# Graph attention on one core: steps of 1024 edges in plain edge order, maxima by a segmented scan

## The chip, the core and the metric

The kernel runs on one core of one Trainium2 chip. A core has five engines that work side by side and meet at semaphores: TensorE (PE; its weight loads are listed apart as PEld), VectorE (DVE), ScalarE (ACT), GpSimd (POOL) and SyncE (SP), which here only issues transfers. The metric is the device time of a run in microseconds; less is better.

## The reference

There are 6250 nodes with 64 features and 206250 edges, sorted by target node `dst`. After a message-passing layer come two graph attention layers of this form (4 heads of 32 channels, then 1 head of 64):

```python
def _gat_layer(x, src, dst, W, a_src, a_dst, b, heads, ch, concat):
    h = (x @ W).reshape(n, heads, ch)
    alpha_src = jnp.sum(h * a_src, axis=-1)
    alpha_dst = jnp.sum(h * a_dst, axis=-1)
    e = alpha_src[src] + alpha_dst[dst]
    e = jnp.where(e > 0, e, NEG_SLOPE * e)
    alpha = _segment_softmax(e, dst, n)
    msg = h[src] * alpha[:, :, None]
    out = jax.ops.segment_sum(msg, dst, num_segments=n)
    return out + b
```

The first part, unchanged but for small pieces, computes per edge `silu(silu([x[src], x[dst], edge_attr, w] @ ew1 + eb1) @ ew2 + eb2)`, sums it by node and applies a small network to the node.

## The kernel before

Nodes stand in 49 buckets of 128, one node on each partition. Edges are worked off in groups of `GE` = 512 edges of one bucket, `U` = 4 on each partition; since each bucket is padded to whole groups there are `GROUPS` = 452.

The program has stages: ordering and placing the edges (to about 450 us), storing the edges' first products at their places by source (`bring` and `put`, to about 2400), the edge network (`edge_mlp`, to about 3950), the node network, and the two attention layers. Each layer is a software pipeline, `attention_pipeline`: every engine has its own `attend(of)`, in which `of(k)` is the group that entered k steps before. Sixteen steps are written out, the rest is a loop with eight steps a round; all engines run through the same number of steps, each at its own pace, and only semaphores hold them together. What an engine does within a step is in the order in which `attend` is written.

For one group of layer 1 the work is as follows.

- SyncE loads the group's ids (`load_ids`). GpSimd gathers the rows of the source nodes from `table0` in HBM with four indirect transfers of 128 rows each (`gather_rows`, L689), into a ring of eight.
- VectorE makes lane numbers and their bits (`edge_codes`, L1464 to L1481) and writes 16 codes beside each gathered row. ScalarE makes from the lane numbers the one-hot matrix edge to node, `a_hot` (L825, L832), and a copy of it in fp32, `a_hot_f` (L857).
- TensorE transposes `a_hot` (L1064) and the codes with the three bf16 parts of the source's shares (L1069), when the rows have landed; ScalarE copies both out of PSUM (L849, L851). A matmul of 512 columns for each head (L1110, `pick`) then shows on every node's partition the shares of its own edges and a very large negative number for all others, and VectorE reduces these to the maxima (`largest_shares`, L1494 in layer 1, L1490 in layer 2).
- VectorE computes the new running shift of the bucket (`new_shifts`, ten short operations), TensorE looks it up for each edge (L1081, twelve small matmuls), VectorE makes the logits (`logits`, four operations), ScalarE the exponentials (L839), VectorE the messages (`messages`, L1580).
- TensorE sums the messages by node with four fp32 matmuls (L1093) of 132 columns, 65 in layer 2; VectorE shrinks the old sum of the bucket and adds the new one (`sums`, L1592 and L1597). The sum goes into one PSUM bank, so each waits until the one before is added (`a_added`).

Semaphores that matter below: `a_hot_ready` (ScalarE), `turned` and `looked_up` (TensorE), `logit_step`, `msg_ready` and `a_added` (VectorE), `exp_ready` (ScalarE).

## Time and profile before

| | us |
|---|---|
| median of 3 runs | 11986.1 |
| lowest and highest | 11957.8, 12015.4 |
| span of the profiled execution | 8886.9 |
| median less span | 3099.2 |
| layer 1 of attention, about | 4062 to 6454 |
| layer 2 of attention, about | 6536 to 8867 |

The span goes from the first to the last instruction that the trace shows. The profile gives no total time of the profiled execution, so the difference to the median is what lies outside its instructions, together with whatever differs between executions. Busy shares are means over stages with different limits, so each stage is read by itself. A clock of 1.00 is TensorE's upper level, 0.50 the lower; values between are a mix in time.

### The profile page before, as it was taken

To read this page: it belongs to the slowest core of one execution; us is meant where nothing else is said; L and a number is where in the kernel's file an instruction comes from. 1 tells how busy PE (TensorE), PEld (TensorE's weight loads), DVE (VectorE), ACT (ScalarE), POOL (GpSimd) and SP (SyncE) were. 2 spreads that over 40 slices of the span, in tenths; PEclk is the share of its full clock that TensorE was granted. 3 is DMA by queue.
4 is the path that set the end of the run, shared out by engine and by line. 5 is a ranking of instruction groups with operands and counts; after the bars stand their busy time and mean duration, and the time that the engine had idled before them with its cause. 6 is when DMAs were issued, how large, how long until landed. Compare 5 with 4: busy or idle time off the path is not lost.

```text
span 8886.9 us, 230055 instructions
## 1 busy us (share of the span) xinstructions
PE 6173.7 (69%) x49885; PEld 5210.5 (59%) x50563; DVE 6168.8 (69%) x25428; ACT 4847.6 (55%) x11854; POOL 6191.5 (70%) x7562
## 2 busy tenths in 40 slices
PE   2466666666599999984666666666646666666665
PEld 2365656556588888873555555545445555656564
DVE  7799833333267676757999999999856666666665
ACT  4133333333245555534777777777647777777775
POOL 0377777777777777735777777777647777777775
PEclk9988888888899999986888888888755555555555
DMA  4233222222232323312222222222421111111114
GB/s 141 52 63 63 62 63 62 63 62 62 61 90 85 86 85 86 85 35 56 55 55 55 55 55 55 56 55 56 47 25 29 29 29 29 29 29 29 29 29 28
DMA packets 990923, 493.64 MB, mean 56 GB/s; under 512 B 830674, under 2 KB 841604, under 8 KB 990276
## 3 DMA queue, kind: packets, MB, share of 16 engines
q0 software_dynamic: 168832, 302.29, 15.6%
q1 hardware_dynamic: 701892, 169.48, 10.2%
q10 hardware_dynamic: 119840, 18.68, 1.3%
q14 instruction: 329, 2.70, 0.1%
q8 instruction: 30, 0.49, 0.0%
HBM read 356.53 MB, written 151.48 MB: 57 GB/s over the span
## 4 chain that ended last, share of the span: by engine, by line
issue 26%; POOL 21%; PE 20%; DVE 15%; DMA 7%; ACT 7%; DVEq 3%; ACTq 1%; POOLq 0%; SPq 0%; another core or an unknown queue 0%
POOL z_s L639 13%; POOL arena L689 8%; DMA arena<-table,arena 6%; PE ps_all L961 5%; PE ps_all L971 5%; ACT arena L825 3%; PE ps_all L984 3%; PE ps_all L981 2%; DVE arena L1494 2%; PE ps_all L1069 1%; ACT arena L857 1%; DVE arena L1580 1%; PE ps_all L993 1%; DVEq L385 1%; DVE ps_all L1232 1%
## 5 line engine op out<-in xcount | busy, mean ns | idle before, releaser
L689 POOL DMA_INDIRECT arena<-table,arena x3616 | 3527.3, 975 | 1421.4 <-issue 963.9
L639 POOL DMA_INDIRECT z_s<-arena x1660 | 1591.9, 959 | 850.8 <-issue 479.6
L1093 PE MATMUL ps_all<-arena 128*128 128x132 f32 (+1 forms) x7232 | 1584.7, 388 | 1.8 <-DVE acc L1597 1.8
L1093 PEld LDWEIGHTS ps_all<-arena 128*128 128x128 f32 x7232 | 1405.9, 288 | 2.7 <-issue 2.6
L1069 PE MATMUL ps_all<-ident_b,arena 128*128 128x128 bf16 x3616 | 465.3, 270 | 1311.8 <-DMA arena<-table,arena 1191.7
L825 ACT ACTIVATE arena<-lanes_b,arena 128x128 bf16<-128x128 bf16 x3616 | 1144.9, 386 | 349.1 <-DVE arena L1467 342.2
L1069 PEld LDWEIGHTS ps_all<-ident_b,arena 128*128 128x128 bf16 x3616 | 282.3, 117 | 1478.6 <-issue 844.4
L1494 DVE TENSOR_REDUCE arena<-ps_all 128x2 f32<-128x1024 f32 x904 | 1098.5, 1215 | 39.0 <-PE ps_all L1110 37.6
L849 ACT ACTIVATE arena<-ps_all 28x512 bf16<-28x512 bf16 (+1 forms) x904 | 527.5, 584 | 956.8 <-PE ps_all L1069 955.8
L744 ACT ACTIVATE arena<-ps_all 18x512 f32<-18x512 f32 x415 | 243.3, 586 | 1211.9 <-PE ps_all L948 1180.1
L1110 PE MATMUL ps_all<-arena,pick 128*128 128x512 bf16 x1809 | 694.6, 489 | 54.6 <-DVE arena L1494 24.3
L1332 DVE CAST arena<-arena 128x4 f32<-128x4 int32 x415 | 72.9, 176 | 875.9 <-DMA z_s<-arena 874.9
L768 ACT ACTIVATE arena<-arena 128x512 f32<-128x512 f32 x452 | 284.9, 630 | 704.6 <-DVE arena L1364 704.6
L946 PE MATMUL ps_all<-ident_b,arena 128*128 128x128 bf16 x1660 | 175.3, 232 | 660.4 <-DVE arena L1325 657.6
L931 PE MATMUL ps_all<-w_edge,arena 128*128 128x128 f32 x3320 | 603.5, 340 | 11.6 <-issue 11.3
L1364 DVE TENSOR_TENSOR arena<-ps_all,b_mid 128x512 f32<-128x512 f32 x452 | 312.4, 691 | 430.5 <-PE ps_all L971 430.5
L1064 PEld LDWEIGHTS ps_all<-ident_b,arena 128*128 128x128 bf16 x3616 | 388.3, 128 | 378.1 <-issue 302.4
L1064 PE MATMUL ps_all<-ident_b,arena 128*128 128x128 bf16 x3616 | 479.9, 274 | 155.9 <-ACT arena L832 106.0
L832 ACT ACTIVATE arena<-arena 128x512 bf16<-128x512 bf16 x904 | 568.8, 629 | 30.6
L931 PEld LDWEIGHTS ps_all<-w_edge,arena 128*128 128x128 f32 x3320 | 532.5, 243 | 72.5 <-issue 43.1
L857 ACT ACTIVATE arena<-arena 128x512 f32<-128x512 bf16 x904 | 553.3, 612 | 0.0
L934 PE MATMUL ps_all<-arena 128*128 x3320 | 545.1, 319 | 0.0
(259 smaller groups left out, 15032.7 us busy)
## 6 DMA issues: line engine op xcount, KB each, us to landing
arena<-z_s SPq DMA_DIRECT2D x452, 264.0 KB, 2.7
arena<-table,arena POOLq DMA_INDIRECT x3616
arena<-rec_d SPq DMA_DIRECT2D x1660, 10.0 KB
z_s<-arena POOLq DMA_INDIRECT x1660
rec_d<-in_rec ACTq DMA_DIRECT2D x1, 16160.0 KB, 59.0
arena<-ids_d SPq DMA_DIRECT2D x904, 4.0 KB
arena<-pos_d SPq DMA_DIRECT2D x830, 0.5 KB
arena<-pos_d ACTq DMA_DIRECT2D x830, 0.5 KB
```

Source lines behind the costliest of these rows:

```text
L639: pool.indirect_dma_start(z_s, bass.IndirectOffsetOnAxis(ap=slot[:, g.slot(SLOTS), u:u + 1], axis=0), z_out[:, g.slot(SLOTS), u, :], None) ...
L689: pool.indirect_dma_start(g_rows[:, r, u * step + CODE_WORDS:(u + 1) * step], None, tables[n], bass.IndirectOffsetOnAxis(ap=ids[:, r, 0, u ...
L825: act.activation(lane_gap[:, g.slot(2), u, :], lanes_b, ACT.Square, bias=neg_lane[:, g.slot(4), u:u + 1]).then_inc(S("lane_gap_ready"), 1)
L832: act.activation(a_hot[:, g.slot(SLOTS)], lane_gap[:, g.slot(2)], ACT.Relu, scale=-1.0, bias=1.0).then_inc(S("a_hot_ready"), 1)
L857: act.activation(a_hot_f[:, g.slot(4)], a_hot[:, g.slot(SLOTS)], ACT.Copy).then_inc(S("a_hot_f_ready"), 1)
L931: pe.matmul(ps[2 + r][:, u * P:(u + 1) * P], x_t[:, g.slot(4), u * P:(u + 1) * P], w_edge, start=(u == 0), stop=False, skip_group_check=True)
L934: mm = pe.matmul(ps[2 + r][:, u * P:(u + 1) * P], own_hot[:, g.slot(4), u, :], own_dst[:, bass.ds(tiles[u], 1), :].rearrange("p a f -> p ( ...
L1064: pe.transpose(bank[:, u * P:(u + 1) * P], a_hot[:, r, u, :], ident_b)
L1069: mm = pe.transpose(bank[:, GE + u * P:GE + (u + 1) * P], g_rows[:, r, u * step:u * step + P // 2].bitcast(BF16), ident_b)
L1093: mm = pe.matmul(ps[6][:, 0:out_w], a_hot_f[:, g.slot(4), u, :], g_msg[:, g.slot(4), u * out_w:(u + 1) * out_w], start=(u == 0), stop=(u = ...
L1110: mm = pe.matmul(bank, picks[n][:, h, :], turned[:, g.slot(SLOTS), 1, :], start=True, stop=True)
L1494: dve.tensor_reduce(part_max[:, g.slot(4), 2 * pair:2 * pair + 2], ps_all[:, pair * 1024:(pair + 1) * 1024].rearrange("p (h e) -> p h e", ...
```

## The change

The edges are no longer padded by bucket. They are taken in plain order in 202 blocks of `BLOCK` = 1024, two halves of 512, `AU` = 8 edges on each partition. A block that holds edges of two buckets is visited once for each; a step of the pipeline is such a visit of block and bucket, `VISITS` = 202 + 48 = 250 a layer. Edges of another bucket have an all-zero row in `a_hot` at that visit.

- SyncE and GpSimd now run by blocks: eight gathers each, into a ring of eight blocks. GpSimd itself waits for the landing of a block, after two gathers of the next, and raises `blocks_in`. SyncE reuses a slot when the last visit of its block is through (`msg_ready`). The node number of each edge stays in SBUF for both layers (`node_of`); before, it was loaded each time.
- In layer 1 codes and `pick` matmuls are gone. VectorE copies the gathered shares (`gathered_shares`), TensorE turns them into 8 rows, half and head, of 512 edges (L1182), VectorE runs a segmented maximum along them (`scan_shares`, L1671, `tensor_tensor_scan` with flags that are very negative at the first edge of a node), TensorE turns the result back (L1194), VectorE keeps it at the last edge of each node (`segment_ends`, L1681), and eight fp32 matmuls of 4 columns bring it to the nodes' partitions (L1218). The flags are computed once, on VectorE in the edge network's stage (`edge_flags`), stored, and read back two transfers a step on ScalarE's queue (`load_flags`).
- Layer 2 keeps codes and `pick`, in 1024 edges at a time.
- The pipelines are shorter: messages four steps behind the start instead of six, and one-hot matrices, transposes and shrink factors have four slots instead of eight, messages two instead of four.

```diff
+AU = HALVES * U
+BLOCK = HALVES * GE
+BLOCK_BITS = 10
+BLOCKS = STORED // BLOCK
+VISITS = BLOCKS + NT - 1
+RING = 8
...
+    return 2 if heads == 1 else 0
...
+        a_hot_f, at = carve(at, [4, AU, P])
+        slot_words = AU * row_words(*LAYERS[0])
+        g_rows, at = carve(at, [RING * slot_words])
+        g_msg, at = carve(at, [2, AU * (F_HID + HEADS)])
...
+                def landed(k):
+
+                    pool.wait_ge(S(f"gathered_{k.slot(LANDING)}"), k.uses(LANDING, 16 * AU))
+                    pool.sem_inc(S("blocks_in"), 1)
...
+                    for u in range(AU):
+                        if u == 2 and k.back(1).exists():
+                            landed(k.back(1))
                         pool.indirect_dma_start(
-                            g_rows[:, r, u * step + CODE_WORDS:(u + 1) * step], None, tables[n],
-                            bass.IndirectOffsetOnAxis(ap=ids[:, r, 0, u:u + 1], axis=0)
-                        ).then_inc(S(f"gathered_{r}"), 16)
-
-                attention_pipeline(pool, 0, gather_rows, n)
+                            g_rows[:, r * slot_words + u * row:r * slot_words + (u + 1) * row], None, tables[n],
+                            bass.IndirectOffsetOnAxis(ap=ids[:, r, u:u + 1], axis=0)
+                        ).then_inc(S(f"gathered_{k.slot(LANDING)}"), 16)
...
+                    g = of(-1)
+                    if n == 0 and g is not None:
+                        load_flags(g)
...
+                        if n == 0:
+                            pe.wait_ge(S("parts_ready"), g.done())
+                            if g.back(1).exists():
+                                pe.wait_ge(S("scanned"), g.back(1).done())
+                            by_u = ps[0][0:HALVES * heads, :].rearrange("k (p u) -> k p u", u=U)
+                            for u in range(U):
+                                mm = pe.transpose(by_u[:, :, u], shares[:, r, u, :], ident)
+                            mm.then_inc(S("shares_turned"), 1)
...
+                    g = of(2)
+                    if g is not None and n == 0:
+                        k = HALVES * heads
+                        pe.wait_ge(S("scanned"), g.done())
+                        if g.back(1).exists():
+                            pe.wait_ge(S("ends_ready"), g.back(1).done())
+                        pe.sem_inc(S("go"), 1)
+                        by_u = running[0:k, g.slot(2), :].rearrange("k (p u) -> k p u", u=U)
...
+                            mm = pe.transpose(ps[1][:, u * k:(u + 1) * k], by_u[:, :, u], ident[0:k, 0:k])
+                        mm.then_inc(S("scan_turned"), 1)
...
+                        for u in range(AU):
+                            mm = pe.matmul(ps[6][:, 0:out_w], a_hot_f[:, g.slot(4), u, :], g_msg[:, g.slot(2), u * out_w:(u + 1) * out_w],
+                                           start=(u == 0), stop=(u == AU - 1))
                         mm.then_inc(S("a_summed"), 1)
...
-                            bank = ps[h] if heads > 1 else ps[g.slot(2)]
-                            mm = pe.matmul(bank, picks[n][:, h, :], turned[:, g.slot(SLOTS), 1, :], start=True, stop=True)
-                            if h % 2 == 1 or heads == 1:
-                                mm.then_inc(S(f"shown{h // 2}"), 1)
...
+                        if n == 0:
+                            pe.wait_ge(S("ends_ready"), g.done())
+                            pe.wait_ge(S("a_hot_f_ready"), g.done())
+                            for a in range(HALVES):
+                                for u in range(U):
+                                    mm = pe.matmul(ps[2][:, a * heads:(a + 1) * heads], a_hot_f[:, g.slot(4), a * U + u, :],
+                                                   largest[:, g.slot(2), u, a * heads:(a + 1) * heads], start=(u == 0), stop=(u == U - 1))
+                        else:
+                            pe.wait_ge(S("codes_turned"), g.fresh().done())
+                            for a in range(HALVES):
+                                mm = pe.matmul(ps[a], pick, turned_codes[:, g.slot(2), a * GE:(a + 1) * GE], start=True, stop=True)
+                        mm.then_inc(S("shown"), 1)
...
+                def gathered_shares(g):
 
...
+                        dve.wait_ge(S("shares_turned" if n == 0 else "turned"), g.back(4).done())
+                    rows = rows_of_visit(g)
+                    dve.wait_ge(S("blocks_in"), (block_of(g) & COUNT_MASK) + (n * BLOCKS + 1))
+                    dve.sem_inc(S("go"), 1)
+                    if n == 0:
+                        dve.tensor_copy(shares[:, r].rearrange("p u (a h) -> p a u h", a=HALVES),
+                                        rows.rearrange("p (a u w) -> p a u w", a=HALVES, u=U)[:, :, :, at_s:at_f]).then_inc(S("parts_ready"), 1)
...
+                def scan_shares(g):
...
-                    for pair in range(heads // 2):
-                        dve.wait_ge(S(f"shown{pair}"), g.done())
-                        dve.tensor_reduce(part_max[:, g.slot(4), 2 * pair:2 * pair + 2],
-                                          ps_all[:, pair * 1024:(pair + 1) * 1024].rearrange("p (h e) -> p h e", h=2),
-                                          op=ALU.max, axis=AX.X).then_inc(S(f"max_taken{pair}"), 1)
-                        yield
+                    k, r = HALVES * heads, g.slot(2)
+                    dve.wait_ge(S(f"flags_in{g.slot(4)}"), g.uses(4, 16 * HALVES))
+                    if g.back(2).exists():
+                        dve.wait_ge(S("scan_turned"), g.back(2).done())
+                    dve.wait_ge(S("shares_turned"), g.done())
+                    dve.tensor_tensor_scan(running[0:k, r, :], flags[0:k, g.slot(4), :], ps[0][0:k, :], -BIG, ALU.add, ALU.max
+                                           ).then_inc(S("scanned"), 1)
...
+                def segment_ends(g):
+
+                    if g is None or n == 1:
+                        return
+                    if g.back(2).exists():
+                        dve.wait_ge(S("shown"), g.back(2).done())
+                    dve.wait_ge(S("scan_turned"), g.done())
+                    dve.scalar_tensor_tensor(largest[:, g.slot(2)].rearrange("p u (a h) -> p (u a) h", a=HALVES),
+                                             ps[1][:, 0:AU * heads].rearrange("p (u h) -> p u h", h=heads), low,
+                                             edges_of_visit(is_last, g).unsqueeze(2).broadcast_to([P, AU, heads]), ALU.subtract, ALU.mult
+                                             ).then_inc(S("ends_ready"), 1)
...
-                    ahead = of(-1)
-                    codes = edge_codes(of(0), ahead) if ahead is not None and ahead.off % 2 == 1 else iter(())
-                    large, shifts = largest_shares(of(3)), new_shifts(of(4))
-                    logs, adds = logits(of(6)), sums(of(8))
-                    for part in (shifts, codes, logs, shifts, adds, logs, shifts, codes, logs, shifts, adds, logs,
-                                 large, shifts, large, shifts):
+                    shifts, logs, adds, codes = new_shifts(of(3)), logits(of(4)), sums(of(6)), edge_lanes(of(0))
+                    for part in (logs, shifts, codes):
                         next(part, None)
-                    messages(of(6))
-                    for part in (shifts, codes, shifts):
+                    segment_ends(of(2))
+                    for part in (logs, shifts, codes, logs, shifts, adds, logs, shifts, codes, adds, shifts):
                         next(part, None)
-
-                attention_pipeline(dve, 8, attend, n, buckets.load)
-                dve.wait_ge(S("a_added"), GROUPS * (n + 1))
+                    scan_shares(of(1))
+                    for part in (shifts, shifts):
+                        next(part, None)
+                    largest_shares(of(2))
+                    messages(of(4))
+                    gathered_shares(of(0))
```

TensorE in attention layer 1 of the kernel before, one step of 512 edges in the steady loop (`ident_b` marks the bf16 transposes, `pick0` the code table, `128x132` the summing matmuls):

```order
L1110 MATMUL ps_all<-arena,pick0 128x512
L1110 MATMUL ps_all<-arena,pick0 128x512 [waits max_taken1]
L1110 MATMUL ps_all<-arena,pick0 128x512
L1062 REGISTER_ALU [waits turned_copied]
L1064 MATMUL ps_all<-ident_b,arena 128x128 [waits a_hot_ready]
L1064 MATMUL ps_all<-ident_b,arena 128x128 x3
L1069 MATMUL ps_all<-ident_b,arena 128x128 [waits gathered_5,high_code_ready,low_code_ready]
L1069 MATMUL ps_all<-ident_b,arena 128x128 x3
L1075 REGISTER_ALU
L1077 REGISTER_ALU [waits max_step]
L1081 MATMUL ps_all<-arena 128x8 [waits logit_step]
L1081 MATMUL ps_all<-arena 128x8 x11
```

TensorE in layer 1 of the changed kernel, one step of 1024 edges (L1182 turns the shares, L1194 turns the scan back, L1205 sums, L1218 is the 4-column matmul that shows the maxima, L1235 the lookups):

```order
L1162 REGISTER_ALU [waits turned_copied]
L1174 MATMUL ps_all<-ident_b,tab 128x128 [waits a_hot_ready]
L1174 MATMUL ps_all<-ident_b,tab 128x128 x7
L1182 MATMUL ps_all<-ident,arena 8x128 [waits scanned,parts_ready]
L1182 MATMUL ps_all<-ident,arena 8x128 x3
L1194 MATMUL ps_all<-ident,arena 128x8 [waits scanned,ends_ready]
L1194 MATMUL ps_all<-ident,arena 128x8 x3
L1205 MATMUL ps_all<-arena 128x132 [waits a_added,msg_ready,a_hot_f_ready]
L1205 MATMUL ps_all<-arena 128x132 x7
L1218 MATMUL ps_all<-arena 128x4 [waits a_hot_f_ready,ends_ready,max_taken]
L1218 MATMUL ps_all<-arena 128x4 x7
L1229 REGISTER_ALU [waits turned_copied]
```

Moved: the four `pick0` matmuls of 512 columns are gone; two groups of fp32 transposes stand before the sum and eight fp32 matmuls of 4 columns behind it, and the transposes no longer wait for the gather but for `parts_ready` and `scanned`, which VectorE raises.

VectorE in layer 1 before, from the last logit steps to the two reductions of 1024 columns:

```order
L1568 TENSOR_TENSOR arena<-arena,ps_all 128x16 [waits logit_step]
L1507 REGISTER_ALU
L1531 TENSOR_TENSOR arena<-shift,arena 128x4 [waits max_step]
L1532 CAST arena<-arena 128x4
L1597 TENSOR_TENSOR acc<-acc,ps_all 128x132 [waits a_shrunk,a_summed]
L1552 REGISTER_ALU
L1571 TENSOR_SCALAR arena<-arena 128x16 [waits logit_step]
L1494 TENSOR_REDUCE arena<-ps_all 128x2 [waits shown0]
L1507 REGISTER_ALU
L1535 TENSOR_SCALAR shift<-arena 128x4 [waits max_step]
L1536 TENSOR_TENSOR arena<-arena 128x4
```

VectorE in layer 1 of the changed kernel, from the end of one step (L1656 copies the gathered shares) to `segment_ends` of the next (L1681):

```order
L1656 ISA
L1656 COPY arena<-arena 128x2x4x4
L1758 TENSOR_TENSOR arena<-arena,ps_all 128x32 [waits looked_up]
L1718 ISA [waits shrink_ready,looked_up]
L1718 TENSOR_SCALAR arena<-dst_parts 128x3x4
L1720 ISA [waits max_taken]
L1720 TENSOR_TENSOR arena<-arena,alpha_d 128x4
L1623 ISA [waits a_hot_ready]
L1623 ISA
L1623 TENSOR_TENSOR arena<-first_node,arena 128x8
L1681 ISA [waits scan_turned,shown]
L1681 SCALAR_TENSOR_TENSOR arena<-ps_all,low,arena 128x32
```

Moved: the reductions of 1024 columns (L1494) are gone from the step; a step now opens with the first logit operation and, two short operations on, stands at L1681 until TensorE has turned the scan of the same step (`scan_turned`).

## Rows read from the trace of the kernel before

**Rows 1.** the page: busy us and share by engine; tenths of 40 slices

```profile
PE 6173.7 (69%) x49885; PEld 5210.5 (59%) x50563; DVE 6168.8 (69%) x25428; ACT 4847.6 (55%) x11854; POOL 6191.5 (70%) x7562
...
POOL 0377777777777777735777777777647777777775
PEclk9988888888899999986888888888755555555555
```

**Rows 2.** stretches of both layers: PE, PEld, DVE, ACT, POOL busy, granted clock, DMA share, GB/s

```profile
5500.00:5750.00 250.00, 168.38 (x1512) 126.63 (x1536) 236.47 (x1035) 177.59 (x483) 190.89 (x195) 0.83 0.27 56
7500.00:7750.00 250.00, 170.99 (x1408) 150.17 (x1432) 157.59 (x998) 176.53 (x493) 189.65 (x199) 0.50 0.20 29
```

**Rows 3.** first and last start of two lines, and the first row of layer 2

```profile
L1464 DVE TENSOR_TENSOR arena<-arena,first_node x452: 151/167/244, 4061.9 to 8825.1; 128x8 int32<-128x8 int32 x151
...
L1614 DVE TENSOR_SCALAR rest<-acc x2: 204/272/340, 6454.4 to 8866.5; 128x196 f32<-128x196 f32 x1, 128x49 f32<-128x49 f32 x1
...
6535.82 0.17 DVE L1464 TENSOR_TENSOR arena<-arena,first_node 128x8 int32<-128x8 int32 x1 [19.85 <-DMA arena<-ids_d]
```

**Rows 4.** GpSimd in order of time in layer 2: start us, us, line, releaser

```profile
7508.31 0.95 POOL L689 DMA_INDIRECT arena<-table,arena  x1 [0.30 <-issue]
7509.57 0.95 POOL L689 DMA_INDIRECT arena<-table,arena  x1 [0.30 <-issue]
```

**Rows 5.** TensorE in order of time, layer 1: two groups, sums of 132 columns

```profile
5502.98 2.11 PE L1093 MATMUL ps_all<-arena 128*128 128x132 f32 x8
...
5507.97 0.97 PEld L1093 LDWEIGHTS ps_all<-arena 128*128 128x128 f32 x8
5507.99 1.15 PE L1093 MATMUL ps_all<-arena 128*128 128x132 f32 x8
```

**Rows 6.** TensorE in order of time, layer 2: sum of 65 columns, one pick

```profile
7504.04 1.78 PEld L1093 LDWEIGHTS ps_all<-arena 128*128 128x128 f32 x8
7504.06 1.95 PE L1093 MATMUL ps_all<-arena 128*128 128x65 f32 x8
...
7505.81 0.63 PE L1110 MATMUL ps_all<-arena,pick 128*128 128x512 bf16 x1
```

**Rows 7.** groups by line and shape: busy us, mean ns

```profile
L1494 DVE TENSOR_REDUCE arena<-ps_all 128x2 f32<-128x1024 f32 x904 | 1098.5, 1215 | 39.0 <-PE ps_all L1110 37.6 <-issue 0.2
...
L1580 DVE TENSOR_TENSOR arena<-arena 128x512 f32<-128x512 f32 x452 | 307.8, 681 | 0.6 <-ACT arena L839 0.6
L948 PE MATMUL ps_all<-ident,arena 128*18 128x128 f32 x1660 | 287.4, 302 | 0.0
...
L1580 DVE TENSOR_TENSOR arena<-arena 128x256 f32<-128x256 f32 x452 | 191.7, 424 | 34.9 <-ACT arena L839 6.0
...
L1232 DVE TENSOR_TENSOR_SCAN ps_all<-acc,carry,ps_all 128x434 f32<-128x434 f32 x147 | 165.5, 1126 | 17.8
...
L1232 DVE TENSOR_TENSOR_SCAN acc<-acc,carry,zero 128x310 f32<-128x310 f32 x49 | 42.3, 864 | 6.0
```

**Rows 8.** VectorE in order of time, layer 1: short operations of one step

```profile
5509.59 0.16 DVE L1525 SCALAR_TENSOR_TENSOR arena<-arena 128x4 f32<-128x4 f32 x1
...
5510.47 0.28 DVE L1597 TENSOR_TENSOR acc<-acc,ps_all 128x132 f32 x1
```

**Rows 9.** layer 2, where a round of eight steps begins on VectorE

```profile
7507.47 0.17 DVE L1520 TENSOR_SCALAR arena<-dst_parts 128x3 bf16 x1 [4.00 <-issue]
```

**Rows 10.** the drain: from VectorE to TensorE

```profile
8861.59 0.23 DVE L1597 TENSOR_TENSOR acc<-acc,ps_all 128x65 f32 x1 [0.50 <-PE ps_all L1093]
...
8861.96 1.94 PE L1093 MATMUL ps_all<-arena 128*128 128x65 f32 x8 [0.41 <-DVE acc L1597]
```

**Rows 11.** ScalarE in order of time, layer 1

```profile
5508.83 0.61 ACT L857 ACTIVATE arena<-arena 128x512 f32<-128x512 bf16 x1
...
5509.45 1.26 ACT L825 ACTIVATE arena<-lanes_b,arena 128x128 bf16<-128x128 bf16 x4
...
5510.74 0.63 ACT L832 ACTIVATE arena<-arena 128x512 bf16<-128x512 bf16 x1
```

519 lines of the change are left out of this document (315 added, 204 removed).

## The prediction

> **What bounds the kernel now.** I read the tenths of the page first, then two stretches of 250 us, then single operations in order of time. The change touches the two attention layers. The first runs from 4061.9 to 6454.4 us, 2392.5 us, the second from 6535.8 to 8866.5, 2330.7 us [rows 3]; each is 452 steps of 512 edges, so 5.29 and 5.16 us a step. In both, GpSimd shows 7 tenths almost without a break [rows 1], and one gather follows the other at 1.26 us, 0.95 of it busy and 0.30 of issue [rows 4]. Four gathers are 5.04 us: GpSimd has no room left in layer 2 (198 gathers fit in 250 us, 199 are there) and little in layer 1 (195), where VectorE is as full, 236.5 of 250 us [rows 2]. So the bound is the gather's issue rate, with VectorE beside it in layer 1. TensorE's granted clock is 0.83 in layer 1, a mix of its two levels, and 0.50 in layer 2, its lower level throughout [rows 2].
>
> **What the change removes.** The gathers fall from 452 x 4 = 1808 a layer to 202 x 8 = 1616. At 1.26 us that is a floor of 2036 us a layer, 8.14 us for each of the 250 steps of 1024 edges. If nothing else came to the front, the layers would take about 2036 + 60 us each, 531 us less than now in sum. The question is whether a step of 1024 edges can pass all engines in 8.14 us.
>
> VectorE's busy time is no obstacle. In layer 1 the step loses two reductions of 1215 ns [rows 7]. It gains a scan of 512: from 310 and 434 columns at 864 and 1126 ns [rows 7], 2.11 ns a column, I get 1.29 us. The message product doubles from 681 ns; with 424 ns at half its size [rows 7] that is 1.0 ns a column, 1.2 us. Some 17 short operations start about 0.1 us apart [rows 8], two of 132 columns take 0.28. In all about 5 us a step. ScalarE has eight squares (four in 1.26 us), three passes over 1024 columns in layer 1 (0.6 us at 512, so about 1.0 each) [rows 11], and two exponentials: 6 us, 7 in layer 2, which has one more copy. Busy shares would allow the gathers' pace.
>
> **The chain of waits in layer 1.** The order of the work does not. Before, transposes and maxima ran several steps ahead of their readers. Now, within one step, these must follow each other:
>
> a. VectorE from L1681 to the second addition into the accumulator, `a_added`: ten operations. The last seven of such a run took 10.47 + 0.28 - 9.59 = 1.16 us [rows 8]; with L1681 and two more, 1.4 us.
> b. To TensorE: 8861.96 - (8861.59 + 0.23) = 0.14 us [rows 10].
> c. Eight summing matmuls instead of four: 2 x 1.15 = 2.3 us at the full clock, 2 x 2.11 = 4.2 us at the half [rows 5].
> d. Then L1218, eight fp32 matmuls of 4 columns on new 128-column weights. No such narrow one is in the trace. At the half clock four sums of 65 columns take 1.95 us and four of 132 take 2.11, with loads of 1.78 busy in the first [rows 5, 6]: width hardly counts there, the loads do. By the loads, 0.97 us for four at full, 1.78 at half [rows 5, 6], eight cost 1.95 or 3.6 us. Below, the cost could go towards 0.1 us if only columns counted; above, to 2.3 or 3.9, as the wide ones. I take the loads, since the 65-wide row lies nearest.
> e. VectorE: reduction 0.15, messages 1.2, copy of the gathered shares 0.2: 1.6 us with the hand-over. The copy comes last in the step, and the next turning waits for it.
> f. TensorE: four transposes of the shares, four of the scan. L948 spends 287.4 / 1660 = 0.173 us on one [rows 7], 1.4 us for eight, and 1.5 with the hand-overs at full; at half I take 1.5 times as much, 2.3 us. Then L1681 of the next step can start.
>
> Sum at the full clock: 1.4 + 0.14 + 2.3 + 1.95 + 1.6 + 1.5 = 8.9 us. At the half clock: 1.4 + 0.14 + 4.2 + 3.6 + 1.6 + 2.3 = 13.2 us. Each round of eight adds something: in layer 2 VectorE stands still for 4.00 us where a round begins [rows 9] and reads its registers anew; about 2.5 us of it is behind TensorE's own work, or 0.3 us a step. So 9.2 to 13.5 us a step, all above 8.14: GpSimd stops being the bound, and waits, through the ring, for the steps.
>
> Which clock? TensorE's wide work now comes in one burst (c), and the rest of the step is narrow matmuls (d, the lookups) and standing still (a, e). Layer 1 before stayed at 0.83 with four 512-column matmuls in each step of 5.3 us, layer 2 at 0.50 with one [rows 2]. The new step has none of them in 9 to 13 us, but sums twice as long. It lies between, nearer to layer 2: I take 12.2 us a step, some 0.7 of the way to the half-clock end. Then layer 1 takes 250 x 12.2 + 80 us to fill and empty = 3130 us, 737 more than now.
>
> **Layer 2** has no scan; two matmuls of 512 columns show the maxima as before. Its chain: VectorE from the step's first operation (it waits for the lookups) through 17 short ones to `a_added`, 2.3; hand-over 0.14; eight sums of 65 columns, 2 x 1.95 less a drain, 3.8; two picks, 0.63 for one and 0.43 for the next, 0.95 beyond the sum's end [rows 6]; one reduction of 1024 columns 1.2 [rows 7]; messages of 512 columns 0.6; copy and hand-over 0.2. That is 9.2 us at the half clock, where this layer is now, and the 4.00 us of each round [rows 9] lie fully on it, 0.5 a step: 9.7 us. Layer 2: 250 x 9.7 + 60 = 2485 us, 154 more. At the full clock the chain would be about 7.7 us and the gathers bound it again.
>
> **The rest.** The flags are made in the MLP stage, about 9 us on VectorE for five passes over 1616 columns (scaled from 1024 columns in 1215 ns [rows 7]), once; its many small transfers run beside that stage. Their price is between 0 and some 50 us; I take 10 in all, with a few microseconds for the minimum of the shares and the smaller tables. GpSimd's wait for the landing of the block before stands behind two further gathers, 2.5 us later; at 12.2 x 250 / 202 = 15.1 us a block against 10.1 of gathers it has 5 us to spare: 0. The two flag transfers a step are issued on ScalarE ahead of its exponentials; ScalarE works 6 of 12.2 us, so they cost 0 too, up to some 6 us each step before that cover is gone.
>
> **The rule on narrow matmuls.** The 65- and 132-column rows say that d is paid by weight loads [rows 5, 6]. The Trainium skill, "TensorE: Matmul & The Clock Gate", section "Step-by-step: what each phase is for", has the array's throughput as purely N cycles and the loads pulled ahead beside the running matmul; by that, d is next to nothing and the full-clock chain 7.0 us. The rows above are against it for fp32 weights.
>
> **Sum.** 8886.9 + 737 + 154 + 10 = 9788 us of span, +901. Between the span and the median, 11986.1, lie 3099.2 us which no row shows; I take them as unchanged: 12887 us. If instead the whole time scaled with the span, the change would be 1.35 times as large, 13202; that is in the range.
>
> **Rivals.**
> 1. *The gathers stay the bound (faster).* If d costs by its columns, the layer 1 chain at the full clock is 8.9 - 1.85 = 7.05 us, 7.4 with the round's turn. With layer 2 also at the full clock, both layers run at 8.14: 11986 - 531 + 10 = 11465 us. It decides where the chain falls under 8.14 us. For it: full gather rows now. Against: the load rows, and layer 2's clock.
> 2. *Clock stays high in layer 1 only.* Layer 1 at 9.2 to 9.7 us a step, 2440 us, +48; layer 2 as above: 11986 + 48 + 154 + 10 = 12198 us. For it: 0.83 now, and longer sums.
> 3. *Half clock throughout.* Layer 1 at 13.5 us: 3455, +1063; with layer 2, 13213 us.
> 4. *The ring does not lead.* If steps wait for gathers after all because slots come free late, a step costs chain plus part of a landing, about 1 us more: 13400 us. Against: eight blocks, of which steps hold four or five.
>
> **Chances.** Forecast 12887 us, 0.50. Rival 1: 0.15; rival 2: 0.17, a part of which (layer 2 also gaining clock) ends below the old time; rival 3: 0.14; rival 4: 0.04. The forecast's own range is 12500 to 13150. For 8 in 10, I leave out most of rival 1 and the far end of 3 and 4: 11900 to 13400. A measurement tells about 0.5% here. Faster by more than that 0.19, within it 0.07, slower 0.74.
>
> **What would show it.** Right, if in layer 1 the gathers no longer follow at 1.26 us but come in groups with idle time, `segment_ends` waits for TensorE's turning of the scan in every step, L1218's loads take about as long as half the sum's at the same clock, steps are 11 to 13 us, and the granted clock lies between 0.5 and 0.75. In layer 2: 0.50, steps near 9.7, and the reduction waiting for the picks. Wrong, if POOL keeps 198 gathers in 250 us (rival 1), or if L1218 takes well under 1 us, or if the clock in layer 1 is above 0.8 (rival 2).

## The result, and the profile of the changed kernel

| on the same chip | median us | lowest to highest |
|---|---|---|
| before, 4 runs | 11976.4 | 11957.8 to 12015.4 |
| changed, 4 runs | 12645.9 | 12629.9 to 12680.6 |

The changed kernel is slower: ratio 1.056, 95% interval 1.053 to 1.058, +669 us. Forecast were 12887 us, +901, in a range of 11900 to 13400. Time and sign lie inside, but the number was put together wrongly, as the experiments show: the profile of before is not one of the timed runs and has none of their slowness.

The first sign is on the page of the changed kernel. Its span is 12639.5 us in an execution of 12641.1 us: nothing lies outside. The rows that answer to [rows 1]:

```profile
PE 7351.6 (58%) x55493; PEld 6470.2 (51%) x55494; DVE 4807.9 (38%) x17947; ACT 4634.8 (37%) x9564; POOL 5747.1 (45%) x7174
...
POOL 0455555555577773434444434441434434344343
PEclk9777777777799997555555555555555555555555
```

GpSimd falls from 7 tenths to mostly 3 or 4 in the layers, as forecast. But it stands at 5, not 7, in the first quarter, the storing of the edge rows, which the change leaves alone. Two stretches of the layers, columns as in [rows 2]:

```profile
6000.00:6250.00 250.00, 164.56 (x1221) 145.31 (x1219) 80.75 (x367) 98.50 (x221) 107.27 (x112) 0.56 0.14 31
10000.00:10250.00 250.00, 121.39 (x1001) 103.17 (x999) 73.36 (x409) 113.92 (x241) 96.75 (x102) 0.50 0.09 14
```

GpSimd issues 112 and 102 gathers in 250 us where [rows 2] have 195 and 199, and no engine is busy for more than two thirds of the time. The clocks, 0.56 and 0.50, are as forecast. From the first to the last `a_added` a layer takes 14.7 us a step, in both layers; forecast were 12.2 and 9.7. One step of layer 1 in order of time (start us, us, engine, line):

```profile
6017.92 3.86 PE L1205 MATMUL ps_all<-arena 128*128 128x132 f32 x16 [1.89 <-DVE acc L1801]
...
6021.57 3.41 PE L1218 MATMUL ps_all<-arena 128*128 128x4 f32 x16
...
6024.84 0.78 PE L1235 MATMUL ps_all<-arena,tab 128*128 128x8 bf16 x24
...
6025.81 0.95 POOL L755 DMA_INDIRECT arena<-table,arena  x1 [0.30 <-issue]
...
6028.33 0.17 DVE L1692 TENSOR_REDUCE arena<-ps_all 128x4 f32<-128x8 f32 x1 [8.94 <-remote]
```

The narrow matmuls (L1218) end at 6024.98. The reduction on VectorE that waits for them (L1692) starts at 6028.33, 3.35 us later; in [rows 10] such a hand-over took 0.14 us. The trace names no engine as its releaser, only "remote". The semaphore events of the trace say what happened: TensorE's increments of `shown` and `looked_up` are registered at 6028.3 and 6028.5, a later one beside them, 1.5 us after GpSimd has ended the issue of the last of eight gathers.

### The profile page after: what moved, and what is told of

Its sections match the earlier page's. It is cut to its first block, busy times and chain, and to the rows that moved or that the text cites. A ratio compares the mean times of both kernels' runs of the same rounds, so it can differ in the third digit from the quotient of the medians.

```text
span 12639.5 us, 214512 instructions
## 1 busy us (share of the span) xinstructions
PE 7351.6 (58%) x55493; PEld 6470.2 (51%) x55494; DVE 4807.9 (38%) x17947; ACT 4634.8 (37%) x9564; POOL 5747.1 (45%) x7174
## 4 chain that ended last, share of the span: by engine, by line
another core or an unknown queue 28%; PE 27%; issue 17%; DVE 8%; ACT 7%; SPq 7%; DVEq 3%; ACTq 2%; DMA 0%
PE ps_all L1205 8%; ACT arena L943 4%; SPq L541 4%; PE ps_all L1057 3%; PE ps_all L1067 3%; PE ps_all L1080 2%; SPq L543 2%; ACT tab L950 2%; PE ps_all L1182 2%; PE ps_all L1077 2%; ACTq L822 1%; PE ps_all L1194 1%; PE ps_all L1165 1%; PE ps_all L1171 1%
## 5 line engine op out<-in xcount | busy, mean ns | idle before, releaser
L755 POOL DMA_INDIRECT arena<-table,arena x3232 | 3096.2, 958 | 4637.5 <-DMA arena<-ids_d 3682.7
L1205 PE MATMUL ps_all<-arena 128*128 128x132 f32 (+1 forms) x8000 | 1869.8, 426 | 1695.2 <-DVE acc L1801 1503.8
L1205 PEld LDWEIGHTS ps_all<-arena 128*128 128x128 f32 x8000 | 1759.6, 331 | 1767.4 <-issue 1481.2
L943 ACT ACTIVATE arena<-lanes_b,arena 128x128 bf16<-128x128 bf16 x4000 | 1214.2, 386 | 107.3 <-issue 63.8
L935 ACT ACTIVATE arena<-tab 128x1024 f32<-128x1024 bf16 x500 | 527.9, 1056 | 1275.4 <-PE ps_all L1205 865.4
L1695 DVE TENSOR_REDUCE arena<-ps_all 128x1 f32<-128x1024 f32 x250 | 306.2, 1225 | 1372.2 <-PE ps_all L1223 1036.8
L1165 PE MATMUL ps_all<-ident_b,tab 128*128 128x128 bf16 x2000 | 258.5, 310 | 925.9 <-ACT tab L950 633.0
L1692 DVE TENSOR_REDUCE arena<-ps_all 128x4 f32<-128x8 f32 x250 | 41.7, 167 | 1801.8 <-remote 1295.6
L1218 PEld LDWEIGHTS ps_all<-arena 128*128 128x128 f32 x4000 | 706.4, 272 | 20.9 <-issue 20.9
L1218 PE MATMUL ps_all<-arena 128*128 128x4 f32 x4000 | 678.6, 302 | 20.6 <-issue 20.6
L1165 PEld LDWEIGHTS ps_all<-ident_b,tab 128*128 128x128 bf16 x2000 | 193.0, 141 | 948.7 <-ACT tab L950 551.6
L1030 PEld LDWEIGHTS ps_all<-arena 128*128 128x128 f32 x3320 | 569.3, 257 | 20.6 <-issue 20.5
L1174 PE MATMUL ps_all<-ident_b,tab 128*128 128x128 bf16 x2000 | 287.9, 305 | 475.8 <-ACT tab L950 238.3
L1235 PEld LDWEIGHTS ps_all<-arena,tab 128*128 128x128 bf16 x12000 | 433.3, 106 | 211.5 <-issue 210.8
L950 ACT ACTIVATE tab<-arena 128x1024 bf16<-128x1024 bf16 x500 | 528.1, 1056 | 18.1
```

The source lines that it names most:

```text
L755: pool.indirect_dma_start(g_rows[:, r * slot_words + u * row:r * slot_words + (u + 1) * row], None, tables[n], bass.IndirectOffsetOnAxis(a ...
L935: act.activation(a_hot_f[:, g.slot(4)], a_hot[:, g.slot(4)], ACT.Copy).then_inc(S("a_hot_f_ready"), 1)
L943: act.activation(lane_gap[:, g.slot(2), u, :], lanes_b, ACT.Square, bias=neg_lane[:, g.slot(4), u:u + 1]).then_inc(S("lane_gap_ready"), 1)
L950: act.activation(a_hot[:, g.slot(4)], lane_gap[:, g.slot(2)], ACT.Relu, scale=-1.0, bias=1.0).then_inc(S("a_hot_ready"), 1)
L1030: mm = pe.matmul(ps[2 + r][:, u * P:(u + 1) * P], own_hot[:, g.slot(4), u, :], own_dst[:, bass.ds(tiles[u], 1), :].rearrange("p a f -> p ( ...
L1165: pe.transpose(bank[:, u * P:(u + 1) * P], a_hot[:, r, u, :], ident_b)
```

## The experiments

Twelve runs were made in four sets, each set on one chip with the kernel before beside it. I call the chip of the result A, the others B to E. On A and B the kernel before takes 11976 and 12275 us, on C, D and E 8904 to 8906 us. No number below can be understood without that, so the chip stands with each. No chip came up twice, so whether the difference belongs to the chip or to the state that it was in, no run shows.

### The kernel before once more (chip B)

> The kernel before, unchanged, profiled once more. The first profile of it had a span of 8886.9 us beside timed runs near 11986 us; the changed kernel's profile has a span of 12639.5 us, which is its whole time, and its unchanged stages (storing the rows, the edge MLP) are longer there than in the first profile of before. Theory 1: the first profile caught an execution unlike the timed ones, and nothing lies outside the span. Then this span is about 11980 us, the layers begin near 5000 us as in the changed kernel, and each layer takes some 3400 us, about 1.5 times what the first profile shows, with TensorE's results arriving late. Theory 2: some 3100 us lie outside the span in this kernel only. Then the span is again near 8890 us and the layers take 2393 and 2331 us.

Measured: 12280.8 us, span 12278.9. Theory 1: nothing lies outside the span. The 8886.9 us of the first profile must then be the whole time of a chip like C to E, where the spans of before are 8896 to 8913 us; the record does not name the chip of that profile. The same moment in layer 1 (VectorE, GpSimd and TensorE in order of time):

```profile
6016.99 0.39 PE L1069 MATMUL ps_all<-ident_b,arena 128*128 128x128 bf16 x4
...
6017.14 0.15 DVE L1467 TENSOR_TENSOR arena<-first_node,arena 128x8 f32<-128x8 int32 x1
6018.06 0.95 POOL L689 DMA_INDIRECT arena<-table,arena  x1 [0.30 <-issue]
6019.32 0.95 POOL L689 DMA_INDIRECT arena<-table,arena  x1 [0.30 <-issue]
6020.58 0.95 POOL L689 DMA_INDIRECT arena<-table,arena  x1 [0.30 <-issue]
6021.84 0.95 POOL L689 DMA_INDIRECT arena<-table,arena  x1 [0.30 <-issue]
6024.52 0.17 DVE L1560 TENSOR_TENSOR arena<-arena,ps_all 128x16 f32<-128x16 f32 x1 [7.22 <-remote]
```

For seven microseconds VectorE and TensorE stand still, and after 6019.27, where ScalarE ends its one-hot matrices, only GpSimd works. These four gathers are the last of eight in a row. TensorE's lookups had ended near 6014.4; their increment and four later ones are registered within 0.3 us of each other, some 1.7 us after the last gather's issue ended, and only then do VectorE and, behind it, TensorE go on. The group from the page, over the whole run:

```profile
L1560 DVE TENSOR_TENSOR arena<-arena,ps_all 128x16 f32<-128x16 f32 (+1 forms) x904 | 144.7, 160 | 2802.3 <-remote 2636.4
```

Of 1233 increments of TensorE between 6000 and 8000 us, 400 come 0.4 to 9 us after the end of their matmul, the middle half of them 1.80 to 1.95 us after the end of the last issue before. In layer 1 of the first profile it is 56 of 2259. From first to last `a_added` a step of 512 edges takes 8.03 and 7.50 us here (layers 1, 2), in the first profile 5.22 and 5.08.

SyncE shows the same chip in another way. One line of its queue in the store stage, the first profile above, chip B below (duration ns min/median/max):

```profile
L469 SPq FUSED_REGOPS  x23: 37/37/37, 1000.1 to 1026.4; - x23
```

```profile
L469 SPq FUSED_REGOPS  x16: 5/37/717, 1001.9 to 1024.8; - x16
```

Of SyncE's 15474 register and semaphore instructions (memory loads left out) some 1880 take about 0.7 us on chip B, none in the first profile.

### Plain loads in place of the gathers (chip B)

```diff
-                    for u in range(AU):
-                        pool.indirect_dma_start(
...
+                    pool.dma_start(g_rows[:, r * slot_words:r * slot_words + AU * row],
+                                   tables[n][0:BLOCK, :].rearrange("(p u) f -> p (u f)", u=AU)
+                                   ).then_inc(S(f"gathered_{k.slot(LANDING)}"), 16)
```

and the same for the kernel before, 512 rows a visit. The stores of the edge rows, which GpSimd issues as indirect transfers too, stay.

> The kernel before, with one plain load of 512 table rows in place of the four indirect gathers of each visit, in both layers; the rows are real but not those of the edges, so the attention is computed on other rows. Theory 1, the gathers bound the layers of before (their issue on GpSimd, and what they hold up): each layer loses over 1000 us and the whole is under 10000 us. Theory 2, the chain of the compute engines bounds it and the gathers are hidden: within 300 us of 11980 us.

Measured: 9270.5 us, 3010 less than before_again. Steps of 5.07 and 4.00 us. Theory 1 holds.

> The changed kernel, with one plain load of 1024 table rows in place of the eight indirect gathers of each block, in both layers; the attention is computed on other rows. Theory 1: the steps are a chain through VectorE and TensorE of about 12 us (layer 1) and 9 us (layer 2) of work, and the further 3 and 6 us a step are completions on TensorE that arrive late only while gathers are being issued; without the gathers the steps fall to 12 and 9 us and the whole to about 12640 - 250 x (3 + 6) = 10400 us. Theory 2: the chain itself takes 15 us in both layers whatever GpSimd does: about 12600 us.

Measured: 11027.1 us, on A it was 12645.9 with gathers. Steps of 12.79 and 10.38 us: the late increments go, as theory 1 has it, but the chain is longer than the 12 and 9 us that it gave.

In both kernels none of TensorE's increments is late in the layers, while in the store stage, which has its indirect transfers still, 577 of 678 are (before_plain, 500 to 3000 us). SyncE's slow instructions, too, are then gone from the layers: of 1028 in before_plain none lies behind 3400 us. So on this chip both come with indirect transfers, and the gathers cost by the late increments, not only by their issue. The second finding matters more for the change. Two steps of before without gathers are 10.1 and 8.0 us, one of the changed kernel 12.8 and 10.4: the chain inside the changed step is longer by 2.7 and 2.4 us, whatever GpSimd does. A chain of waits sets the step, as forecast; which chain, this pair does not tell.

### VectorE's order (chip B)

```diff
-                    largest_shares(of(2))
                     messages(of(4))
                     gathered_shares(of(0))
+                    largest_shares(of(2))
```

> The changed kernel with three calls of VectorE's round in another order: the messages and the copy of the gathered shares stand ahead of the reduction that waits for the largest shares, not behind it. Theory 1, the chain inside a step of layer 1 sets its length: the 1.23 us of the messages, the 0.17 us copy and the share transposes (about 1.0 us) behind them leave the chain, up to 2.4 us of 15 a step, 250 steps: 600 us off layer 1, and 0.7 + 0.2 us a step, 200 us, off layer 2; about 11850 us. Theory 2, the late completions on TensorE set the step: under 200 us in all.

Measured: 13085.3 us, ratio to before 1.065 (1.063 to 1.067), more than the changed kernel's 1.056 on A. Steps of 16.87 and 14.01 us, on A it was 14.7 and 14.7: neither theory has a loss. The changed kernel itself did not run on B, so the loss is no comparison on one chip. The next set shows why nothing is gained. More increments are late here (333 of 696 between 6000 and 8000 us, in the changed kernel on A 197 of 807); that this makes the loss is likely but not shown.

### Shorter runs of gathers (chip C)

```diff
                         if u == 2 and k.back(1).exists():
                             landed(k.back(1))
+                        if u == AU // 2:
+                            pool.wait_ge(S(f"gathered_{k.slot(LANDING)}"), k.uses(LANDING, 16 * AU) - 16 * AU // 2)
+                            pool.sem_inc(S("go"), 1)
```

The kernel before gets a wait for the four gathers of the last visit ahead of the next four.

> The kernel before, with one wait more on GpSimd: the four gathers of a visit are issued only when the four of the visit before have landed. In the ordinary execution of before a visit takes 8.03 us in layer 1 and 7.50 in layer 2 where 5.07 and 4.00 do without the gathers, and TensorE's increments arrive in a burst some 1.8 us after the last of eight gathers in a row. Theory 1, TensorE's increments are held while gathers are issued back to back, and go out in the first pause of about 1.8 us: the pause now comes after four gathers, not eight; a visit costs at most 4 x 1.26 + 1.8 = 6.8 us, less than now, although GpSimd waits more: 452 x (1.2 + 0.7) = 850 us off, a ratio near 0.93. Theory 2, the issue of the gathers is the bound and the late increments only follow from it: every pause is added to a visit, so the kernel gets slower, by up to 452 x 2 x 1 us, a ratio of 1.03 to 1.08.

> The changed kernel, with one wait more on GpSimd: the last four of a block's eight gathers are issued only when its first four have landed. Theory 1, as for the kernel before: a held increment waits at most for four gathers and their landing, 6.8 us, not 12; layer 1 goes from 14.7 us a step towards the 12.8 us that it takes without gathers but is now held by GpSimd at 2 x 6.8 = 13.7, layer 2 from 14.7 to 13.7: about 400 to 500 us off the 1.056 ratio, so 1.01 to 1.02. Theory 2: the pauses are added, 1.8 us a step, and the ratio is 1.08 to 1.10.

Measured: before_paced 10785.6 us, ratio 1.212 (1.210 to 1.214); after_paced 10120.8 us, ratio 1.137 (1.135 to 1.139). But chip C is of the other sort: before takes 8905.6 us there, and of 1391 increments of before_paced between 5000 and 7000 us one is late. So the question of the runs' length stayed open. What the pair shows is another thing. Where nothing is late, the wait makes before slower by 1880 us: its steps go to 7.21 and 7.22 us, which is GpSimd's new pace, four issues and a landing. GpSimd's group between 5000 and 6000 us:

```profile
L692 POOL DMA_INDIRECT arena<-table,arena x557 | 531.7, 955 | 470.6 <-DMA arena<-table,arena 335.3 <-issue 135.3
```

In the changed kernel the same pauses cost nothing: 12.84 and 10.39 us a step, as without gathers. Its gathers are covered.

### What lies on the chain of a step (chip C)

```diff
-                                for u in range(U):
+                                for u in range(U - 1, U):
                                     mm = pe.matmul(ps[2][:, a * heads:(a + 1) * heads], a_hot_f[:, g.slot(4), a * U + u, :],
-                                                   largest[:, g.slot(2), u, a * heads:(a + 1) * heads], start=(u == 0), stop=(u == U - 1))
+                                                   largest[:, g.slot(2), u, a * heads:(a + 1) * heads], start=True, stop=True)
```

> The changed kernel with plain loads for gathers, and of the eight narrow matmuls that bring the segment maxima to the lanes only the last of each half (2 of 8), so that most maxima are left out. The prediction puts the eight on the chain of a step of layer 1 at 1.95 us (full clock) to 3.6 us (half clock). On the chain and at the half clock: 12.8 us a step falls by 0.75 x 3.4 = 2.6 us to 10.2, 640 us in all. If VectorE or ScalarE (its selection work is 5.2 us a step) bound the step instead: under 0.5 us a step. Layer 2 is not changed.

> The changed kernel with plain loads for gathers and VectorE's messages and share copy ahead of its reduction of the largest shares. Without gathers a step of the changed kernel takes 12.8 us in layer 1 and 10.4 in layer 2. If the chain is the one of the prediction, the messages (1.23 us, layer 2 0.68) and the copy (0.17) leave it: layer 1 to 11.0 to 11.6 us, layer 2 to 9.6 us; whole time 11027 less 300 to 600 us. If a step is bound by TensorE's own work in order (about 10.8 us at the low clock) with fixed gaps, or if another wait comes last, under 100 us.

Measured: 10034.1 and 10042.8 us. Against 12.79 us with the full chain (after_plain, chip B), layer 1 takes 12.66 and 12.76 a step, with a median of 12.77 and 12.78. Neither edit is worth more than 0.13 us a step, where 2.6 and at least 1.2 were expected if the forecast's chain led. In one_narrow_plain the narrow matmuls do shrink:

```profile
6014.31 0.72 PE L1215 MATMUL ps_all<-arena 128*128 128x4 f32 x4
6014.55 1.06 ACT L932 ACTIVATE arena<-tab 128x1024 f32<-128x1024 bf16 x1 [3.38 <-PE ps_all L1202]
```

0.72 us in place of 3.41, and the step keeps its length. The second row says where it runs: ScalarE has waited 3.38 us for the sum (L1202 there).

### The ring through ScalarE, cut (chip D)

The changed kernel on chip D, one step of layer 1 in order of time:

```profile
6009.10 3.86 PE L1205 MATMUL ps_all<-arena 128*128 128x132 f32 x16 [1.88 <-DVE acc L1801]
...
6012.53 3.54 PEld L1218 LDWEIGHTS ps_all<-arena 128*128 128x128 f32 x16
6012.75 3.41 PE L1218 MATMUL ps_all<-arena 128*128 128x4 f32 x16
...
6013.00 1.06 ACT L935 ACTIVATE arena<-tab 128x1024 f32<-128x1024 bf16 x1 [3.10 <-PE ps_all L1205]
6013.96 2.43 ACT L943 ACTIVATE arena<-lanes_b,arena 128x128 bf16<-128x128 bf16 x8
...
6016.20 0.17 DVE L1692 TENSOR_REDUCE arena<-ps_all 128x4 f32<-128x8 f32 x1 [5.73 <-PE ps_all L1218]
...
6016.42 1.06 ACT L950 ACTIVATE tab<-arena 128x1024 bf16<-128x1024 bf16 x1
...
6017.47 0.17 DVE L1656 COPY arena<-arena 128x32 f32 x1
...
6017.53 1.04 PE L1174 MATMUL ps_all<-ident_b,tab 128*128 128x128 bf16 x8 [0.72 <-ACT tab L950]
...
6018.36 1.06 PE L1182 MATMUL ps_all<-ident,arena 128*8 128x128 f32 x4
...
6019.35 0.64 PE L1194 MATMUL ps_all<-ident,arena 8*128 8x8 f32 x4
6020.22 0.25 DVE L1681 SCALAR_TENSOR_TENSOR arena<-ps_all,low,arena 128x32 f32<-128x32 f32 x1 [2.28 <-PE ps_all L1194]
...
6021.45 0.28 DVE L1801 TENSOR_TENSOR acc<-acc,ps_all 128x132 f32 x1
...
6021.88 1.44 PE L1205 MATMUL ps_all<-arena 128*128 128x132 f32 x5 [1.88 <-DVE acc L1801]
```

`a_hot_f` has four slots, is made one step behind the start of the pipeline and read by the sum five steps behind, so the copy that makes it (L935) waits for the sum of the same round (L1205), and ScalarE's squares (L943) and `a_hot` (L950) are queued behind the copy. TensorE's transposes (L1174) wait for `a_hot`, the share turnings stand behind them, and `a_added` (L1801) lets the next sum start at 6021.88. Round it goes: 3.90 + 0.96 + 2.46 + 1.11 + 2.69 + 1.66 = 12.78 us. The forecast's ring is in the same rows: sum and narrow matmuls 6009.10 to 6016.16, VectorE to 6017.64, shares 6018.36 to 6020.22, VectorE to 6021.73, hand-over 0.15. That is 12.1 us, 0.7 shorter: it waits. And this is a step with the narrow matmuls at the half clock. In 131 of the 250 steps of this run they take 2.3 us or less, and the step keeps its length all the same: a median of 12.80 us, against 12.78 where they take 3.4. So the shorter ring has 0.7 us to spare in one half of the steps and about 2 us in the other, which is why cutting either of its terms did nothing.

In layer 2 the ring through ScalarE is there too: sum, copy, squares, `a_hot`, the two groups of transposes, after which the next sum starts.

```profile
8505.67 3.68 PE L1205 MATMUL ps_all<-arena 128*128 128x65 f32 x16
...
8509.39 1.06 ACT L935 ACTIVATE arena<-tab 128x1024 f32<-128x1024 bf16 x1 [1.69 <-PE ps_all L1205]
...
8510.35 2.43 ACT L943 ACTIVATE arena<-lanes_b,arena 128x128 bf16<-128x128 bf16 x8
...
8512.81 1.06 ACT L950 ACTIVATE tab<-arena 128x1024 bf16<-128x1024 bf16 x1
...
8513.92 1.03 PE L1165 MATMUL ps_all<-ident_b,tab 128*128 128x128 bf16 x8 [3.10 <-ACT tab L950]
...
8514.89 1.04 PE L1171 MATMUL ps_all<-ident_b,arena 128*32 128x128 bf16 x8
```

```diff
-                        if g.back(4).exists():
-                            act.wait_ge(S("a_summed"), g.back(4).done())
-                        act.activation(a_hot_f[:, g.slot(4)], a_hot[:, g.slot(4)], ACT.Copy).then_inc(S("a_hot_f_ready"), 1)
...
                         act.activation(a_hot[:, g.slot(4)], lane_gap[:, g.slot(2)], ACT.Relu, scale=-1.0, bias=1.0
                                        ).then_inc(S("a_hot_ready"), 1)
+
+                    g = of(1)
+                    if g is not None:
+                        if g.back(4).exists():
+                            act.wait_ge(S("a_summed"), g.back(4).done())
+                        act.activation(a_hot_f[:, g.slot(4)], a_hot[:, g.slot(4)], ACT.Copy).then_inc(S("a_hot_f_ready"), 1)
```

In three_moves, besides, on VectorE:

```diff
-                    for part in (logs, shifts, codes):
+                    for part in (adds, logs, shifts, codes, adds):
                         next(part, None)
                     segment_ends(of(2))
-                    for part in (logs, shifts, codes, logs, shifts, adds, logs, shifts, codes, adds, shifts):
+                    for part in (logs, shifts, codes, logs, shifts, logs, shifts, codes, shifts):
...
-                    largest_shares(of(2))
                     messages(of(4))
                     gathered_shares(of(0))
+                    largest_shares(of(2))
```

> The changed kernel, unchanged, beside the kernel before on one chip. Chips differ: before took 11976 and 12275 us on two of them and 8906 us on a third, where its profile has no late increments and its GpSimd issues without gaps. On a chip of the first sort: steps of 14.5 to 15.5 us, ratio 1.05 to 1.06. On one of the second: steps of 12.8 and 10.2 to 10.4 us as with the plain loads, 8906 us + 250 x (12.8 + 10.4) - 452 x (5.22 + 5.08) = 10050 us, ratio 1.12 to 1.14.

> The changed kernel with ScalarE's copy of a_hot to a_hot_f (1.06 us) at the end of its round, behind the eight squares and the making of the next a_hot. Without gathers a step of layer 1 takes 12.78 us whether six of the eight narrow matmuls are left out or not and wherever VectorE's messages stand, so the prediction's chain is not the longest. Theory 1, the ring runs through ScalarE: sum (3.8), copy, which waits for the sum to free its buffer (1.06), squares (2.4), a_hot (1.06), then transposes, shares, scan transposes (2.7), VectorE to a_added (1.5). Moving the copy takes 4.5 us of ScalarE out of the ring; what is then late is the ring of the prediction, sum, narrow matmuls and VectorE, 12.3 to 12.4 us at the half clock: 0.4 us a step of layer 1 and 1 to 2 us a step of layer 2, 300 to 600 us off after_again. Theory 2, the steps are bound by TensorE and the order on ScalarE is indifferent: within 50 us of after_again.

> As copy_last, and on VectorE the addition to the accumulator stands ahead of the segment ends, and messages and share copy ahead of the reduction of the largest shares. If both rings are as read, neither is left and a step of layer 1 is TensorE's own work in its order, 1.0 + 1.0 + 0.6 + 3.9 + 3.4 + 0.8 = 10.7 us at the half clock, less if the busier engine gets the full one; layer 2 near the 8 x 1.26 = 10.1 us of the gathers: 500 us less than copy_last's gain leaves, about 900 us off after_again on a chip without late increments. If late increments rule (a chip of the first sort), the gain over after_again is smaller, 200 to 500 us. If a third ring of 12 us exists, no gain over copy_last.

| chip D | median us | ratio to before (95%) | us a step, layer 1, 2 |
|---|---|---|---|
| before | 8903.7 | | 5.22, 5.08 for 512 edges (first profile) |
| after_again | 10099.1 | 1.134 (1.132 to 1.136) | 12.82, 10.39 |
| copy_last | 9250.1 | 1.039 (1.037 to 1.041) | 10.95, 8.87 |
| three_moves | 8608.9 | 0.968 (0.965 to 0.971) | 9.16, 8.14 |

One moved copy is worth 849 us where 300 to 600 were expected. Layer 2 gives 1.52 us a step, as expected (1 to 2); layer 1 gives 1.87 where 0.4 was expected. The expectation took the forecast's ring at the half clock in every step. On average over the steps the narrow matmuls took only 2.68 us in after_again, and now take 2.12, in 216 of 250 steps 2.3 or less; the granted clock of layer 1 is 0.64, 0.57 in after_again. With 2.12 in place of 3.41 the forecast's ring comes to 10.8 us, beside the 10.95 measured, so it now leads. The two moves on VectorE are worth another 641 us, 1490 in all where some 900 were expected. Part of that is a slip of the expectation: 10.1 us for eight gathers is the time of a block, and a step of layer 2 has 202 / 250 of a block, 8.14 us. With all three moves TensorE has no gap in a step of layer 1:

```profile
6011.36 3.41 PE L1221 MATMUL ps_all<-arena 128*128 128x4 f32 x16
...
6013.38 1.04 ACT L954 ACTIVATE arena<-tab 128x1024 f32<-128x1024 bf16 x1
...
6014.63 0.78 PE L1238 MATMUL ps_all<-arena,tab 128*128 128x8 bf16 x24
...
6015.27 1.01 PE L1177 MATMUL ps_all<-ident_b,tab 128*128 128x128 bf16 x8
...
6016.08 1.06 PE L1185 MATMUL ps_all<-ident,arena 128*8 128x128 f32 x4
...
6017.07 0.64 PE L1197 MATMUL ps_all<-ident,arena 8*128 8x8 f32 x4
...
6017.64 3.89 PE L1208 MATMUL ps_all<-arena 128*128 128x132 f32 x16
```

and in layer 2 the bound of the forecast's first paragraph on the change is reached, 8.14 us a step, with GpSimd as full as in [rows 2]:

```profile
7500.00:7750.00 250.00, 210.82 (x1741) 185.49 (x1770) 134.73 (x744) 199.20 (x431) 190.01 (x198) 0.50 0.19 28
```

> The kernel of three_moves once more, for another chip. On a chip where before takes about 8900 us: 8610 us and a ratio of 0.965 to 0.971, as measured. On a chip of the other sort, where before takes 12000 us and TensorE's increments arrive late while GpSimd issues gathers: the store and MLP stages cost 1000 us more for either kernel, and if the late increments cost a shorter ring as much as a long one (1.9 and 4.3 us a step of layer 1 and 2 in after), 8610 + 1000 + 250 x 6.2 = 11160 us, a ratio of 0.91 to 0.95; if increments wait for the end of each run of eight gathers whatever the ring is, the steps go to about 12 us of gathers and landing plus the work behind it, 14 to 15 us as in after, and the ratio to 1.03 to 1.05.

Measured on chip E: 8574.9 us, before 8904.1, ratio 0.963 (0.961 to 0.964), a little under the expected 0.965. It was again a chip of the faster sort, so what the moves do where increments are late stays open. On D and E this version beats the kernel before by over 3%, and on D the changed kernel by 15%; on A or B it was not measured.

## Why the prediction came out right

**What bounds before.** Half right. Where nothing is late, taking the gathers away shortens a step from 5.22 to 5.07 us in layer 1 and from 5.08 to 4.00 in layer 2 (with gathers from the first profile, without from before_plain): GpSimd bounds layer 2, VectorE layer 1, and the rows showed both at the edge. On chip B a third thing rules, the late increments; on A before was not profiled, but its time and the changed kernel's trace say the same.

**The 3099 us outside the span.** Wrong in kind. The forecast took the span of one execution and the median of others, and read their difference as a constant. It is the difference between two sorts of chip: each profile whose total time is known has under 3 us outside its span (1.6 in the changed kernel's). It neither stayed constant nor grew with the work, as the forecast's second thought had it, but fell: before takes 3073 us more on A than on D, the changed kernel 2547.

**The terms of the chain**, at the half clock, from the step of chip D shown above:

| term | forecast us | measured us |
|---|---|---|
| a, VectorE from L1681 to `a_added` | 1.4 | 1.51 |
| b, hand-over | 0.14 | 0.15 |
| c, eight sums | 4.2 | 3.65 to the first narrow one |
| d, eight narrow matmuls | 3.6 | 3.41 |
| e, VectorE from L1692 to the copy | 1.6 | 1.44 |
| f, share and scan turnings to L1681 | 2.3 | 1.86 |
| the ring | 13.2 | 12.1 |

The terms hold within a fifth. That narrow fp32 matmuls are paid by their weight loads is shown: eight of four columns take 3.41 us at the half clock, with 3.54 of loads beside them, and 1.85 at the full one in the changed kernel's trace, against 3.6 and 1.95 by the load rows. The Trainium skill, "TensorE: Matmul & The Clock Gate", section "Step-by-step: what each phase is for", has throughput as purely N cycles; for these weights the trace, with 3.41 us for 32 columns in all, does not agree.

**The step that failed** is the list of what must follow what. It read VectorE's and TensorE's queues and took ScalarE's 6 us of 12 as cover. It left out that L935 waits for the sum of its own round, which puts 4.5 us of ScalarE into a ring of 12.78 us. The forecast of 12.2, a mean of two clocks on the wrong ring, was near this by chance. Its clock was right, 0.56 and 0.57 measured in layer 1 and 0.50 in layer 2, but the narrow matmuls' clock does not move the ring that leads (12.80 and 12.78 us, above). The same holds for layer 2, 9.7 forecast, 10.39 measured, with the same ring (sum 3.7, ScalarE 4.5, two groups of transposes 1.9).

**The sum.** On a chip without late increments +901 was forecast and +1195 measured: layer 1 from first to last `a_added` 3193 us against 2352 (+841, forecast +737), layer 2 2587 against 2291 (+297, forecast +154), the rest, with the longer filling of the pipelines, +58 by difference (forecast +10). On chip A it was +669, 526 less, which is just what the 3073 and 2547 us above differ by. Where the 526 come from, the traces tell roughly. In the layers, late increments cost before 2.8 and 2.4 us on each of 452 steps (B against the first profile), 2364 us, and the changed kernel 1.9 and 4.3 us on each of 250 (A against after_plain), 1536 us: it has fewer steps in which to wait, and gives back 828 us. Before is 299 us slower on B than on A; if all of that lies in the layers, 529 are left. This is an estimate across chips, and before was not profiled on A. So two errors met: a chain forecast too cheap by 294 us, and a cost of before, 526 us larger than that of the changed kernel, that the profile did not show. That they run against each other is luck; on a chip where nothing is late, the change costs +1195 and not the +901 of the forecast.

**Rivals.** The gathers did not stay the bound (1), the clock was 0.57 in layer 1, not above 0.8 (2). Rival 3 had everything at the half clock in each step: the sum mostly was (3.8 us or more in 195 of 250 steps on D), the narrow matmuls in half of the steps only, and its ring is 12.1 us, not 13.2. Rival 4 is excluded where nothing is late, by after_paced and after_plain: covered gathers cost nothing.

## What to carry to other kernels

Before a chain is summed, go through every buffer with few slots and ask which step's reader frees it: a copy that waits for this round's sum puts everything queued behind it on its engine into the ring, and an engine that is busy half the time is no cover for that. A ring that is a little longer hides the other, so cutting a term of the shorter shows nothing; cut the wait that the rows name, then look for the next. And where span and median lie far apart, settle which execution the profile shows before a single term is costed.

## What the runs showed of the hardware

- One and the same kernel takes 8904 to 8906 us on three chips and 11976 and 12275 us on two others, each within 0.5%. The difference lies where GpSimd issues indirect transfers. On chip B a third of TensorE's increments in before's layer 1 (400 of 1233 between 6000 and 8000 us) arrive 0.4 to 9 us late, in a burst some 1.8 us after a row of gathers has been issued; in the first profile it is 56 of 2259. Without gathers (before_plain, after_plain, on chip B) none is late in the layers. In the store stage, where GpSimd scatters rows, 566 of 674 increments between 500 and 3000 us are late on chip B. Why two sorts of chip differ so, and through what an increment is held, no run shows.
- On chip B some 1880 of SyncE's register and semaphore instructions take 0.7 us in place of 0.03 to 0.04, and of those on chip A some 1090; about half of B's lie in the store stage, most of A's. Without gathers those of the layers are gone (before_plain, chip B).
- Eight fp32 matmuls of 4 columns, each on new 128-column weights, take 3.41 us at the half clock and 1.84 at the full one; 24 bf16 matmuls of 8 columns take 0.78 us in the same step (chip D).
- Whether shorter rows of gathers help where increments are late was not settled: the set that should tell ran on a chip of the other sort, where the extra wait costs the kernel before 21%.
